# Keys and queries made inside the first gradient's program, Newton-Schulz with an early norm and without a rebuilt X

## The chip, the cores and the metric

The kernel runs on one core of a Trainium2 chip. The time is device microseconds (us) of one execution, the median of several. Five engines work side by side, each in its own order: TensorE (PE in the profile, its weight loads PEld), VectorE (DVE), ScalarE (ACT), GpSimd (POOL) and SyncE (SP, which only issues transfers here). They wait for each other by semaphores.

## What is computed

A hybrid transformer block on x of shape 4 x 512 x 128, so 2048 tokens, 16 tiles of 128. The change touches only the first of its four parts, a test-time-training attention:

```
q, k, v = split(layernorm(x) @ qkv_w + qkv_b)            # each 2048 x 128
q, k = q / (norm over 8 + 1e-6) * scale + bias           # 16 heads of 8
theta = gate, val (128 x 512), proj (512 x 128)
for _ in range(2):
    h = swish(k @ gate) * (k @ val); pred = h @ proj
    grads = d mean((pred - v)**2) / d theta
    theta -= 0.1 * newton_schulz(grads)                  # 3 matrices
o = (swish(q @ gate) * (q @ val)) @ proj @ proj_w + proj_b

newton_schulz(G): X = G / (norm(G) + 1e-7)
    5 times: A = X @ X.T; X = a*X + (b*A + c*(A @ A)) @ X
```

Then follow a mixture of 8 small experts, a block-causal attention and the experts again, which stay as they are.

## The kernel before

The program is a row of blocks; at the end of each all engines meet. `qkv_phase` makes q, k, v. Then, twice, `gradient_phase` and `schulz_phase`, and then `query_phase`.

**qkv_phase.** Each engine runs `pipeline`: step s does stage X of tile s minus its lag. ACT normalises a tile, PE turns and projects it (L315, L320), DVE adds the bias (`bias_add`, L348), ACT squares, DVE sums the squares of each head (L352), ACT takes the root and DVE inverts it, POOL multiplies by it (`unit`, L254) and by the scale (`scaled`, L261), DVE adds the shift (L367), PE turns the result (L325, L326) and ACT copies it to `qkT` and to `qkv`. Ahead of the first tile ACT copies a transposed `proj` (L269, L270) and only then loads the table for the layer norm's root (L179).

**gradient_phase.** All products with the weights of `forward` and `back` are three matmuls each (`mm3`): an operand is split into a part `h` that a fast format holds and the rest `l`. ACT makes `kh` from `qkT` and POOL the rest `kl`, per tile and again in each of the two gradients. PE's order for a step is turn_h, add_proj, forward, predict, add_gate, turn_d, add_val, back, with lags of 1 to 3 tiles; ACT does tanh, derive and two copies, DVE seven elementwise operations. Three PSUM banks (`acc`) gather the gradients.

**schulz_phase.** The three gradients (index m) go side by side. With P = c A A + b A + a I, an X that isn't touched gives X' = P X and A' = P A P. So the kernel keeps A (128 x 128) and a product Q of the Ps. A round is: square (PE), poly (DVE), times_a (PE), a copy T (ACT), next_a (PE), a mixture and a copy (DVE). After two rounds it rebuilds X and its transpose with Q (L695, L699), takes A from them anew (L653), and goes on with three rounds. Ahead of this the norm of G is read from the diagonal of G G^T, and X is turned by PE and copied by ACT. At its end gate, val and proj are updated and split again, with POOL making the rests of gate and val (L646).

**query_phase.** Splits q as above (`high`, `low`), 512 tokens at a time, and runs gate and up products (`gate_up`), a sigmoid, and an output product.

## Time and profile before

| | |
|---|---|
| median of 3 runs | 866.35 us (862.17 to 867.6) |
| the profiled execution | 866.14 us |
| its span, first to last instruction | 863.7 us |
| mean granted TensorE clock | 0.94 of full speed |
| PE, PEld busy | 90%, 71% |
| DVE, ACT, POOL busy | 63%, 46%, 31% |

The stages lie so in the span: q, k, v from 0 to 51.2 us; first gradient to 159.9; first Newton-Schulz to 196.0; second gradient to 306.7; second Newton-Schulz to 342.7; query to 393.7; the rest to 863.7. A busy time is the sum over a stretch; a share near 100% says that an engine had always something in work, not that it ran at its peak. In a timeline row the text in brackets is the idle time just before and what ended it. An fp32 product is recorded as two matmuls, so `x6` are three products.

### The profile page before, as it was taken

What the parts mean: (1) busy time and instruction counts of PE and PEld (TensorE: products, weight loads), DVE (VectorE), ACT (ScalarE), POOL (GpSimd) and SP (SyncE); (2) the same over time, 40 slices, a digit from 0 to 9 for tenths busy, and PEclk for the clock granted to TensorE, in tenths of its full rate; (3) what the DMA queues carried; (4) which work ended last, traced back from release to release, by engine and by line L of the source; (5) the groups of instructions that cost most, each with busy time, mean ns of one, the idle gap of its engine ahead of it and who ended that gap; (6) DMA issues with size and microseconds to landing.
All of it is one profiled execution on the core that took longest, in us unless ns stands there. A gap on an engine that the chain in (4) does not pass through costs nothing. (4 is left out here: it accounts for less than half of the span.)

```text
span 863.7 us, 15529 instructions
## 1 busy us (share of the span) xinstructions
PE 774.2 (90%) x5512; PEld 616.6 (71%) x5512; DVE 545.4 (63%) x1649; ACT 394.9 (46%) x1118; POOL 270.7 (31%) x476
## 2 busy tenths in 40 slices
PE   3669999897999988987858999999999999999786
PEld 1239999775999976677645677777777777777765
DVE  3945656444555535664796776776677666665468
ACT  4733333243333234312255766565556555564224
POOL 4830000002445002100372444343334333333027
PEclk9969999997999999895898999999999999999678
DMA  3040000000000000000000000000000000000001
GB/s 104 1 134 1 1 2 1 1 1 1 1 1 2 1 1 1 0 1 1 0 2 0 2 2 2 2 2 1 2 2 1 2 2 2 2 1 2 1 0 50
DMA packets 9466, 7.17 MB, mean 8 GB/s; under 512 B 1584, under 2 KB 9008, under 8 KB 9264
## 3 DMA queue, kind: packets, MB, share of 16 engines
q1 hardware_dynamic: 9392, 6.19, 2.3%
q8 instruction: 46, 0.75, 0.4%
q14 instruction: 28, 0.23, 0.1%
HBM read 5.14 MB, written 1.05 MB: 7 GB/s over the span
## 5 line engine op out<-in xcount | busy, mean ns | idle before, releaser
L1295 POOL TENSOR_SCALAR t_p_<-t_p_,t_rinv_ 128x128 f32<-128x128 f32 (+3 forms) x256 | 132.1, 532 | 202.3 <-DVE t_rinv_ L1491 202.3
L1325 ACT ACTIVATE t_p_<-t_p_,t_nmin_ 128x128 f32<-128x128 f32 (+3 forms) x256 | 140.0, 551 | 9.1 <-DVE t_nmin_ L1484 9.1
L1484 DVE CUSTOM_DVE_ANT_0 t_p_<-t_S_,t_mask_ 128x128 f32<-128x128 f32 (+3 forms) x256 | 112.8, 487 | 21.7 <-PE t_S_ L1382 17.3
L1330 ACT ACTIVATE t_pT_<-t_T_ 128x384 f32<-128x384 f32 (+1 forms) x96 | 50.5, 526 | 118.3 <-PE t_T_ L1394 118.3
L1394 PEld LDWEIGHTS t_T_<-ident,t_p_ 128*128 128x128 f32 x640 | 68.2, 141 | 44.9 <-issue 26.0
L1382 PE MATMUL t_S_<-t_k_,t_q_ 64*128 64x256 f32 (+3 forms) x512 | 95.0, 468 | 0.1
L1394 PE MATMUL t_T_<-ident,t_p_ 128*128 128x128 f32 x640 | 90.8, 281 | 0.3 <-ACT t_pT_ L1330 0.3
L1409 PEld LDWEIGHTS t_O_<-t_pT_,t_v_ 128*64 128x64 f32 x1280 | 69.2, 137 | 11.0 <-ACT t_pT_ L1330 10.5
L1409 PE MATMUL t_O_<-t_pT_,t_v_ 128*64 128x128 f32 x1280 | 76.9, 275 | 0.0
L522 DVE SCALAR_TENSOR_TENSOR g_sw<-g_th,g_G 128x512 f32<-128x512 f32 x32 | 22.0, 688 | 71.3 <-ACT g_slope L436 66.2
L1382 PEld LDWEIGHTS t_S_<-t_k_,t_q_ 64*128 64x128 f32 x512 | 41.5, 185 | 26.9 <-DVE t_nmin_ L1484 12.3
L1495 DVE COPY t_pT_<-t_T_ 128x384 f32<-128x384 f32 (+1 forms) x96 | 57.3, 597 | 1.4 <-PE t_T_ L1394 1.3
L408 POOL TENSOR_TENSOR g_kl<-qkT,g_kh 128x128 fp32r<-128x128 f32 x32 | 14.6, 457 | 138.0 <-ACT g_kh L427 138.0
L1500 DVE COPY t_oT_<-t_O_ 128x512 f32<-128x512 f32 x32 | 22.1, 691 | 54.8 <-PE t_O_ L1409 54.8
L1325 ACT ACTIVATION_READ_ACCUMULATOR t_p_<-t_p_,t_nmin_ 128x1 f32 x256 | 48.6, 190 | 0.0
L440 ACT ACTIVATE g_hT<-g_H 128x512 f32<-128x512 f32 x32 | 19.1, 597 | 60.0 <-PE g_H L472 60.0
L1037 ACT ACTIVATE m_y_<-m_A_,m_wt_ 128x128 f32<-128x128 f32 x96 | 28.0, 367 | 25.4 <-PE m_A_ L102 25.4
L646 POOL TENSOR_TENSOR gvl<-gv,gvh 128x512 fp32r<-128x512 f32 x4 | 5.0, 1273 | 104.3 <-ACT gvh L751 104.3
L479 PEld LDWEIGHTS g_PT<-proj,g_hT 128*128 128x128 f32 x256 | 33.8, 193 | 2.6
L498 PE MATMUL acc<-qkv,g_dg 128*128 128x128 f32 x256 | 34.0, 276 | 1.0 <-DVE g_dg L549 1.0
L479 PE MATMUL g_PT<-proj,g_hT 128*128 128x128 f32 x256 | 34.1, 276 | 0.0
L498 PE MATMUL acc<-qkv,g_du 128*128 128x128 f32 x256 | 33.8, 275 | 0.0
(259 smaller groups left out, 1794.5 us busy)
## 6 DMA issues: line engine op xcount, KB each, us to landing
wqkv<-in_L_attn_b_w_qkv_dram SPq DMA_DIRECT2D x1, 1536.0 KB
x<-in_L_attn_a_x_dram SPq DMA_DIRECT2D x4, 256.0 KB, 4.2
out_dram<-x SPq DMA_DIRECT2D x4, 256.0 KB, 2.3
we<-in_L_ffn_We_dram SPq DMA_DIRECT2D x1, 512.0 KB
wout<-in_L_attn_b_w_out_dram SPq DMA_DIRECT2D x1, 512.0 KB
proj<-n_L_attn_a_ttt_proj_dram SPq DMA_DIRECT2D x1, 256.0 KB, 5.3
gv<-n_L_attn_a_ttt_gate_dram SPq DMA_DIRECT2D x1, 256.0 KB, 4.9
gv<-in_L_attn_a_ttt_val_dram SPq DMA_DIRECT2D x1, 256.0 KB, 5.4
```

Source lines behind the costliest of these rows:

```text
L479: last = pe.matmul(pred, hT[:, t.ring, n * P:n * P + P], self.proj[:, n, :], start=(n == 0), stop=(n == NC - 1))
L498: last = pe.matmul(self.acc[:, n, m, :], src[:, t.ring, m * P:m * P + P], d[:, t.ring, :] if n == 2 else k, start=False, stop=False, skip_ ...
L1037: last = act.activation(y[:, t % 4, tile_of(k)], experts_of(t, e), ACT.Copy, scale=weight(t, e))
L1295: last = pool.tensor_scalar(pr[:, G.par, h, cols], pr[:, G.par, h, cols], rinv[:, G.par, n:n + 1], 1.0, ALU.mult, ALU.mult)
L1325: act.activation(pr[:, G.par, h, cols], pr[:, G.par, h, cols], ACT.Exp, bias=nmin[:, G.par, n:n + 1], scale=-1.0, accum_out=rsum[:, G.par, ...
L1330: act.activation(pT[:, G.par, 0, G.blocks], psT[:, 0, 0:G.width], ACT.Copy).then_inc(t["eA"], 1)
L1382: last = pe.matmul(psS[:, (2 * G.n + h) % 3, at_:at_ + (qt + 1) * P], qp[d, G.par, qt * P:qt * P + P], kp[d, G.par, 0:(qt + 1) * P], start ...
L1394: last = pe.transpose(psT[:, h, k:k + P], pr[:, G.par, h, at_:at_ + P], ident[:, :])
L1409: last = pe.matmul(psO[d, qt * P:qt * P + P], v[:, G.b % 2, n, G.p * P + h * DH:G.p * P + h * DH + DH], pT[:, G.par, h, at_:at_ + P], star ...
L1484: dve.tensor_tensor_reduce(pr[:, G.par, h, cols], psS[:, (2 * G.n + h) % 3, at_:at_ + keys], mask[:, SEQ - keys:SEQ], 1.0, -NEG, ALU.add, ...
L1495: dve.tensor_copy(pT[:, G.par, 1, G.blocks], psT[:, 1, 0:G.width]).then_inc(t["eB"], 1)
L1500: dve.tensor_copy(oT[:, b % 2, p, :], psO[:, :]).then_inc(t["oT"], 1)
```

## The change

Four things change. (1) `qkv_phase` is gone; a class `Front` does its work inside the first gradient's block, and its buffers are those of the gradient. ACT no longer copies `proj` ahead of the layer norm. POOL squares 6 of the 16 tiles, root and inverse are taken for 4 tiles at once, and POOL alone does the product with the inverse, the scale and the shift, in place in `qkv`. (2) The transposes of q and k (`turn_qk`) are a stage of the gradient's own pipeline, all other lags are one larger, and ACT (`high`) and DVE (`low`) split both once into `qkh` and `qkl`, which the second gradient and the query stage read. (3) In `schulz_phase` all five rounds run on A; Q is gathered beside them in a PSUM bank of its own; X is turned inside the rounds. A round's square and mixture become A times R with R = c A + b I, and a I is added on DVE. The norm comes from the squares of G, on ACT and DVE. (4) The activation table of the next stage is loaded in `schulz_phase`, and the second `schulz_phase` leaves out the updates that nobody reads (`proj`, `pTh`, `pTl`).

```diff
+class Front:
+    POOL_SQUARES = tuple(range(4, NT, 2))
...
+        def square(t):
+            pool.wait_ge(self.s["out"], t + 1)
+            pool.wait_ge(self.s["ss"], t - 3)
+            qk = k.qkv[:, t, 0:2 * P]
+            pool.tensor_tensor(self.sq[:, t % 4, :], qk, qk, ALU.mult).then_inc(self.s["sqp"], 1)
+        def unit(t):
+            heads = lambda ap: ap.rearrange("p (g d) -> p g d", d=QD)
+            qk = k.qkv[:, t, 0:2 * P]
+            pool.wait_ge(self.s["inv"], t // TPB + 1)
+            pool.tensor_tensor(heads(qk), heads(qk), self.ssq[:, t, :].unsqueeze(2).broadcast_to([P, 2 * QH, QD]),
+                               ALU.mult).then_inc(self.s["m"], 1)
+            pool.wait_ge(self.s["m"], t + 1)
+            pool.tensor_tensor(qk, qk, self.scale_all[:, :], ALU.mult).then_inc(self.s["s"], 1)
+            pool.wait_ge(self.s["s"], t + 1)
+            pool.tensor_tensor(qk, qk, self.shift_all[:, :], ALU.add).then_inc(self.s["k"], 1)
+        early = 0
+        for t in self.POOL_SQUARES:
+            square(t)
+            if t in (8, 12):
+                unit(early)
+                early += 1
+        for t in range(early, NT):
+            unit(t)
+            if t == early + 1:
+                pool.wait_ge(self.s["ptc"], 2)
+                pool.tensor_tensor(k.pTl[:, :], k.projT[:, :], k.pTh[:, :].bitcast(F32), ALU.subtract).then_inc(self.s["ptl"], 1)
...
+        def root(b):
+            of = slice(b * TPB, b * TPB + TPB)
+            act.wait_ge(self.s["ss"], TPB * (b + 1))
+            act.activation(self.ssq[:, of, :], self.ssq[:, of, :], ACT.Sqrt).then_inc(self.s["rt"], 1)
+        def keep_proj():
+            act.wait_ge(self.s["pt"], 1)
+            for dst in (k.projT, k.pTh):
+                act.activation(dst[:, :], self.psP[:, :, :].rearrange("p c d -> p (c d)"), ACT.Copy).then_inc(self.s["ptc"], 1)
+        for s in range(NT + 3):
+            if s < NT:
+                norm(s)
+            if 0 <= s - 1 < NT:
+                copy(s - 1)
+            if 0 <= s - 3 < NT and s - 3 not in self.POOL_SQUARES:
+                square(s - 3)
+            if s == NT:
+                keep_proj()
+            if s % TPB == 3 and TPB < s < NT:
+                root(s // TPB - 1)
+        take_first()
+        root(BATCH - 1)
...
+        def sumsq(t):
+            dve.wait_ge(*self.squares(t))
+            dve.tensor_reduce(self.ssq[:, t, :], self.sq[:, t % 4, :].rearrange("p (g d) -> p g d", d=QD),
+                              AX.X, ALU.add).then_inc(self.s["ss"], 1)
+        def invert(b):
+            of = slice(b * TPB, b * TPB + TPB)
+            dve.wait_ge(self.s["rt"], b + 1)
+            dve.tensor_scalar(self.ssq[:, of, :], self.ssq[:, of, :], 1e-6, None, ALU.add).then_inc(self.s["gd"], 1)
+            dve.wait_ge(self.s["gd"], b + 1)
+            dve.reciprocal(self.ssq[:, of, :], self.ssq[:, of, :]).then_inc(self.s["inv"], 1)
+        for s in range(NT + 3):
+            if 0 <= s - 1 < NT:
+                bias_add(s - 1)
+            if 0 <= s - 3 < NT:
+                sumsq(s - 3)
+            if s % TPB == 0 and s >= 2 * TPB:
+                invert(s // TPB - 2)
+        invert(BATCH - 1)
...
-                pipeline(act, (2, keep_hT), (0, k_high), (1, tanh), (1, derive), (2, dT_high))(base)
+                if front:
+                    act.sem_inc(g["hT"], 1)
+                    front.scalar(act, lambda: high(Tile(0, 0)))
+                    act.preload_act_table(ACT.Derivative_silu)
+                    pipeline(act, (3, keep_hT), (2, tanh), (2, derive), (3, dT_high), (1, next_high))(base)
+                else:
+                    pipeline(act, (2, keep_hT), (1, tanh), (1, derive), (2, dT_high))(base)
...
+                def turn_qk(t):
+                    pe.wait_ge(front.s["k"], t.done())
+                    pe.wait_ge(front.s["ptc"], 2)
+                    if t.number() != 0:
+                        pe.wait_ge(g["qkl"], t.done() - 1)
+                    for n in range(2):
+                        last = pe.transpose(turned[:, n, :], qkv[:, t.number(), n * P:n * P + P], self.ident[:, :])
+                    last.then_inc(g["T"], 1)
...
-                pipeline(pe, (2, turn_h), (3, add_proj), (1, forward), (2, predict), (3, add_gate), (2, turn_d),
-                         (3, add_val), (2, back))(base)
+                if front:
+                    pipeline(pe, (3, turn_h), (4, add_proj), (2, forward), (3, predict), (4, add_gate), (3, turn_d),
+                             (4, add_val), (3, back), (1, turn_qk))(base)
...
+                def low(t):
+                    dve.wait_ge(g["qkh"], t.done())
+                    dve.tensor_tensor(qkl[:, :, t.cols()], turned, qkh[:, :, t.cols()].bitcast(F32), ALU.subtract).then_inc(g["qkl"], 1)
...
+                    pipeline(dve, (2, swish), (3, error), (2, hidden), (3, dT_low), (2, gate_factor), (3, grad_val),
+                             (1, low), (3, grad_gate))(base)
...
+                gram(0)
+                gram(1)
+                pe.wait_ge(self.s_trace, 3 * step + 3)
+                pe.matmul(total, self.ones[:, :], tr[:, :], start=True, stop=True).then_inc(self.s_total, 1)
+                gram(2)
+                for k in range(K - 1):
+                    poly(k)
+                    times_a(k)
+                    if k < 3:
+                        turn(k)
+                    if k:
+                        gather(k)
+                    next_a(k)
+                poly(K - 1)
+                gather(K - 1)
...
-                square(0)
-                times_a(0)
-                next_a(0)
-                square(1)
-                last_q(1, lambda m: Pm[:, 0, m, :])
-                for m in range(3):
-                    pe.wait_ge(used[m], after(m, "q1"))
-                    for n in range(NC):
-                        last = pe.matmul(big[m][:, n, :], X[:, m, n, :], Q[:, m, :], start=True, stop=True)
-                    last.then_inc(made[m], 1)
-                for m in range(3):
-                    pe.wait_ge(used[m], after(m, "xt2"))
-                    pe.matmul(flat(big[m]), Q[:, m, :], flat(X[:, m, :, :]), start=True, stop=True).then_inc(made[m], 1)
-                for m in range(3):
-                    pe.wait_ge(used[m], after(m, "x2"))
-                    gram(m, XT2, "a2").then_inc(made[m], 1)
-                square(2)
-                times_a(2)
-                next_a(2)
-                square(3)
-                times_a(3, True)
-                next_a(3)
-                square(4)
-                last_q(4, lambda m: Q[:, m, :])
...
+                act.activation(junk[:, 0, :], flat(big[0]), ACT.Square, accum_out=tr[:, 0:1]).then_inc(self.s_trace, 1)
                 act.preload_act_table(ACT.Sqrt)
+                act.wait_ge(self.s_total, step + 1)
+                act.activation(nrm[:, :], total, ACT.Sqrt).then_inc(self.s_root, 1)
+                act.preload_act_table(ACT.Derivative_silu if again else ACT.Sigmoid)
+                act.wait_ge(self.s_nsv, 3 * step + 3)
                 for m in range(3):
-                    copy(m, flat(X[:, m, :, :]), flat(big[m]), "x")
-                act.wait_ge(self.s_norm, 4 * step + 4)
-                act.activation(nrm[:, :], small[0][:, 3, 0:3], ACT.Sqrt).then_inc(self.s_root, 1)
...
+                for k in range(K - 1):
+                    take(T, 2, f"t{k}")
+                    if k:
+                        take_q(k)
+                    take(A, 0, f"a{k}")
+                    if k < 3:
+                        take_x(k)
+                take_q(K - 1)
...
+                def factor(name):
+                    for m in range(3):
+                        dve.wait_ge(used[m], in_sbuf(name))
+                        dve.scalar_tensor_tensor(R[:, m, :], A[:, m, :], NS_C, bI[:, :], ALU.mult, ALU.add).then_inc(r_used[m], 1)
...
+                        dve.wait_ge(made[m], in_psum(f"p{k}"))
+                        dve.tensor_tensor(Pm[:, k % 2, m, :], small[m][:, 1, :], aI[:, :], ALU.add).then_inc(used[m], 1)
...
-                act.preload_act_table(ACT.Sigmoid)
...
-                        last = mm3(pe, ps_[:, n % 2, :], self.gvh[:, cols], self.gvl[:, cols], qh[:, b.ring, :], ql[:, b.ring, :])
+                        last = mm3(pe, ps_[:, n % 2, :], self.gvh[:, cols], self.gvl[:, cols],
+                                   self.qkh[:, 0, b.cols(SEQ)], self.qkl[:, 0, b.cols(SEQ)])
...
-            k.qkv_phase()
```

How the order moves at three places (L520 is predict, L541 the three add stages, L526 turn_d, L504 turn_qk, L513 turn_h in the changed file).

PE in the middle of the first gradient, before, from predict of one tile to turn_h of the next:

```order
L479 MATMUL g_PT<-proj,g_hT 128x128 x4
L498 MATMUL acc<-qkv,g_dg 128x128 x4
L485 MATMUL g_PT<-ident,g_d 128x128
L498 MATMUL acc<-qkv,g_du 128x128 x4
L100 MATMUL g_D<-pTh,g_dTh 128x512
L101 MATMUL g_D<-pTl,g_dTh 128x512
L102 MATMUL g_D<-pTh,g_dTl 128x512
L472 MATMUL g_H<-ident,g_h 128x128 x4
```

and in the changed kernel:

```order
L520 MATMUL g_PT<-proj,g_hT 128x128 x4
L541 MATMUL acc<-qkv,g_dg 128x128 x4
L526 MATMUL g_PT<-ident,g_d 128x128
L541 MATMUL acc<-qkv,g_du 128x128 x4
L100 MATMUL g_D<-pTh,g_dTh 128x512
L101 MATMUL g_D<-pTl,g_dTh 128x512
L102 MATMUL g_D<-pTh,g_dTl 128x512
L504 MATMUL g_PT<-ident,qkv 128x128 x2
L513 MATMUL g_H<-ident,g_h 128x128 x4
```

Two transposes per tile have moved from their own stage to the end of PE's step.

POOL in the front of the changed kernel (L179 squares, L185 product with the inverse, L188 scale, L190 shift):

```order
L179 TENSOR_TENSOR g_du<-qkv 128x256 x3
L185 TENSOR_TENSOR qkv<-qkv,g_ssq 128x256
L188 TENSOR_TENSOR qkv<-qkv,g_scale_all 128x256
L190 TENSOR_TENSOR qkv<-qkv,g_shift_all 128x256
L179 TENSOR_TENSOR g_du<-qkv 128x256 x2
L185 TENSOR_TENSOR qkv<-qkv,g_ssq 128x256
L188 TENSOR_TENSOR qkv<-qkv,g_scale_all 128x256
L190 TENSOR_TENSOR qkv<-qkv,g_shift_all 128x256
L179 TENSOR_TENSOR g_du<-qkv 128x256
```

The squares are those of tiles 4, 6 and 8, then 10 and 12, then 14; between them stand the three operations of tile 0 and of tile 1. Before, POOL had two operations a tile (L254, L261) and no squares.

PE in Newton-Schulz, the changed kernel, start and first two rounds (L726 poly, L731 times_a, L720 turn, L738 gather, L744 next_a):

```order
L714 MATMUL n_small<-n_XT 128x128 x8
L749 MATMUL n_side<-n_tr,ones 128x3
L714 MATMUL n_small<-n_XT 128x128 x4
L726 MATMUL n_small<-n_R,n_A 128x128 x3
L731 MATMUL n_small<-n_A,n_P 128x128 x3
L720 MATMUL acc<-ident,n_XT 128x128 x4
L744 MATMUL n_small<-n_T,n_P 128x128 x3
L726 MATMUL n_small<-n_R,n_A 128x128 x3
L731 MATMUL n_small<-n_A,n_P 128x128 x3
L720 MATMUL acc<-ident,n_XT 128x128 x4
L738 MATMUL n_side<-n_P 128x128 x3
L744 MATMUL n_small<-n_T,n_P 128x128 x3
```

The transposes of X and the product for Q now stand between times_a and next_a, and the three rows of the rebuild (L695, L699, L653) are gone.

## Rows read from the trace of the kernel before

**Rows 1.** Engine busy time by stretch: start, end and length in us, then busy time.

```profile
0.00:51.20 51.20, 24.56 (x84) 11.95 (x84) 32.76 (x105) 29.47 (x101) 34.77 (x47) 0.92 0.15 44
...
159.90:196.00 36.10, 29.81 (x190) 24.98 (x190) 17.39 (x62) 13.86 (x34) 2.50 (x2) 0.95 0.00 1
...
342.70:393.70 51.00, 43.66 (x232) 36.45 (x232) 31.76 (x56) 13.51 (x22) 5.87 (x4) 0.90 0.00 0
```

**Rows 2.** Timeline before the first bias addition: start, duration in us, engine, line.

```profile
9.29 0.17 DVE L170 TENSOR_SCALAR lnw<-lnw 128x16 f32<-128x16 f32 x1
...
11.70 1.28 ACT L179 ACT_TABLE_LOAD   x1
...
12.99 0.22 ACT L181 ACTIVATE lnw<-lnw 128x16 f32<-128x16 f32 x1
...
14.25 0.88 ACT L276 ACTIVATE p_xn_<-x,p_nmr_,rstd 128x128 f32<-128x128 f32 x2 [1.04 <-DVE p_nmr_ L338]
...
17.49 0.56 DVE L348 TENSOR_TENSOR qkv<-p_Q_,p_bias_ 128x384 f32<-128x384 f32 x1 [3.43 <-PE p_Q_ L320]
```

**Rows 3.** Instruction groups of the first 51.2 us: count, busy us, mean ns.

```profile
L261 POOL TENSOR_TENSOR p_sc_<-p_m_,p_scale_all_ 128x256 f32<-128x256 f32 x16 | 14.2, 893 | 0.0
...
L254 POOL TENSOR_TENSOR p_m_<-qkv,p_inv_ 128x256 f32<-128x256 f32 x16 | 10.8, 672 | 3.7 <-DVE p_inv_ L361 1.7
...
L348 DVE TENSOR_TENSOR qkv<-p_Q_,p_bias_ 128x384 f32<-128x384 f32 x16 | 8.1, 504 | 4.3 <-PE p_Q_ L320 4.3
...
L352 DVE TENSOR_REDUCE ssq<-p_sq_ 128x32 f32<-128x256 f32 x16 | 6.4, 397 | 0.0
```

**Rows 4.** Timeline of PE, first forward matmul of the first gradient.

```profile
53.55 0.77 PE L100 MATMUL g_G<-gvh,g_kh 128*128 128x512 f32 x1 [0.26 <-issue]
```

**Rows 5.** Timeline, first gradient in steady state: one tile's period and a DVE operation.

```profile
69.55 0.60 PE L472 MATMUL g_H<-ident,g_h 128*128 128x128 f32 x4
...
75.83 0.60 PE L472 MATMUL g_H<-ident,g_h 128*128 128x128 f32 x4
...
76.27 1.06 PE L498 MATMUL acc<-g_d,g_h 128*128 128x128 f32 x8
...
151.45 0.69 DVE L545 SCALAR_TENSOR_TENSOR g_du<-g_D,g_sw 128x512 f32<-128x512 f32 x1 [0.47 <-PE g_D L102]
```

**Rows 6.** Timeline of the first Newton-Schulz stage: its start, rounds and last product.

```profile
160.10 1.08 ACT L723 ACTIVATE n_XT<-acc 128x512 f32<-128x512 f32 x2 [5.08 <-PEq L383]
...
167.64 0.94 PE L659 MATMUL n_small<-n_A 128*128 128x128 f32 x6 [2.52 <-DVE n_T L778]
...
173.16 2.94 PE L695 MATMUL acc<-n_Q,n_X 128*128 128x128 f32 x24
...
182.00 0.94 PE L659 MATMUL n_small<-n_A 128*128 128x128 f32 x6 [0.64 <-DVE n_T L778]
...
183.40 0.72 ACT L723 ACTIVATE n_T<-n_small 128x128 f32<-128x128 f32 x3 [4.08 <-PE n_small L666]
...
183.73 0.94 PE L671 MATMUL n_small<-n_T,n_P 128*128 128x128 f32 x6
...
184.80 1.28 PE L659 MATMUL n_small<-n_A 128*128 128x128 f32 x6
...
190.22 2.31 PE L713 MATMUL acc<-n_X,n_Q 128*128 128x512 f32 x5
```

**Rows 7.** Timeline of PE, first forward matmul of the second gradient.

```profile
198.34 0.76 PE L100 MATMUL g_G<-gvh,g_kh 128*128 128x512 f32 x1 [1.11 <-ACT g_kh L427]
```

**Rows 8.** Timeline around the start of the query stage.

```profile
339.52 2.50 POOL L646 TENSOR_TENSOR gvl<-gv,gvh 128x512 fp32r<-128x512 f32 x2 [52.15 <-ACT gvh L751]
...
342.85 1.28 ACT L850 ACT_TABLE_LOAD   x1 [1.69 <-PEq L629]
...
342.89 1.68 PE L872 MATMUL q_W_<-proj_w,projT 128*128 128x128 f32 x8 [2.29 <-PEq L629]
...
345.97 0.79 PE L100 MATMUL q_G_<-q_qh_,gvh 128*128 128x512 f32 x1 [1.40 <-DVE q_ql_ L907]
```

544 lines of the change are left out of this document (237 added, 307 removed).

## The prediction

> **What bounds the kernel now.** I read first the busy times by stretch [rows 1]. The stretch of q, k and v (0 to 51.2 us) is half idle on every engine: PE 24.56 us, DVE 32.76, ACT 29.47, POOL 34.77 of 51.2, so waits between engines bound it. In the first Newton-Schulz stretch PE is busy 29.81 of 36.1 us, but with chains of three small products. In the query stretch PE has 43.66 of 51.0. Then the timeline at the places where the stages start. The first bias addition runs at 17.49 [rows 2]; the first forward product of the gradient at 53.55 [rows 4]. In the gradient one tile takes 75.83 - 69.55 = 6.28 us on PE without a gap [rows 5]: there PE is the bound, and work taken from other engines gives nothing. In Newton-Schulz a round with nothing beside it takes 184.80 - 182.00 = 2.80 us, while from 173.16 to 182.00, 8.84 us, X is rebuilt [rows 6]. The sum is made against the profiled execution, 866.14 us, 0.2 below the median of 866.35.
>
> **1. The front, to the first forward product.** ACT loaded the root's table at 11.70, behind the two copies of proj, and took the root at 12.99; its input was there at 9.29 + 0.17 and a semaphore, about 9.66 [rows 2]. The changed kernel loads the table at the very start and has nothing ahead of the root, so all that follows moves by 12.99 - 9.66 = 3.3 us: the first normalised tile from 14.25 to 10.9, the first bias addition from 17.49 to 14.2 [rows 2]. A tile costs DVE 0.504 + 0.397 = 0.90 us [rows 3]; ACT has less than before. So the bias of tile 8 is added 8 x 0.90 = 7.2 us later, plus about 1.5 for the first slow tiles and the first inversion: done at 22.9.
>
> From there POOL is the chain, because it has its tasks in a fixed order and DVE and ACT wait for its squares. Four squares (tiles 8, 10, 12, 14) and the operations of tiles 0 and 1 stand there. A square I price at 0.75, between the product with the inverse (0.672) and the one with the scale (0.893) [rows 3]; the three operations of a tile at 2.35, between 3 x 0.672 = 2.0 and 3 x 0.893 = 2.7, nearer the middle because one is of the first kind and two of the second, which slows only beside DVE. With 0.5 us of waiting for the bias of tile 12: 22.9 + 3.0 + 4.7 + 0.5 = 31.1. Then two sums of squares on DVE (0.8), the root on ACT (0.3), a wait of DVE for POOL to finish one operation and a short add (0.7), a reciprocal over 128 columns (0.45, between the sum's 0.397 and the bias addition's 0.504 [rows 3]) and the rest `low` of tile 0 (0.5): the first forward product at 33.9. Against 53.55 [rows 4] that is **-19.7 us**. The transposes of tile 0, the copies of proj and `high` are done by then, in ACT's and PE's waits; the table for tanh loads under the first forward product. The ends: with every POOL operation at 0.672 and no wait 32.2, so -21.3; with every one at 0.893 and twice the waits 37, so -16.5. What becomes late next is POOL's rest: tile 2 comes at about 33.5, then one tile in 2.35 us, while the gradient takes one in 6.5; pTl on POOL is ready at 37, `back` of tile 0 needs it at 43.
>
> **2. The first gradient.** PE gets two transposes a tile, each 0.11 us, for four take 76.27 - 75.83 = 0.44 [rows 5]. 0.22 x 14 tiles (the first two fall into gaps of the start) is **+3.1 us**. ACT's `kh`, POOL's `kl` go and ACT's `high`, DVE's `low` come: neither engine is the bound, 0. If that cover fails, see the last rival.
>
> **3. Newton-Schulz, twice.** Counted from its first copy (160.10), the first square product started at 167.64 - 160.10 = 7.5 us, the last product with X at 190.22 - 160.10 = 30.1 [rows 6]. Now: ACT's two copies 1.1 and its square 0.8, a table load 1.28, so the root ends at 3.3, while DVE's two sums end at 2.4 and the total is there at 3.0. A second table load ends at 4.6 (on the path, DVE's three small operations lie under it). Three copies of 128 columns take ACT 0.72 [rows 6], so one 0.28 and each further one 0.22. A copy of A 0.3, R on DVE 0.3: the first product at 5.25. A phase of three products, whose result another engine must take, lasts (183.73 - 182.00)/2 = 0.87 us; from product to ACT's copy 183.40 - 182.87 = 0.53, and from there 0.33 to the next product [rows 6] (182.87 being the middle of the two phases). Round 0: poly 0.87; times_a 0.66 and the turn of X 0.44, together 1.1; next_a, copy of A, R 1.2; in all 3.2. Rounds 1 and 2: 0.87; times_a 0.66, turn 0.44, gather 0.66, together 1.76; then ACT copies three Qs (0.9 from the last product of gather) before A, and A and R take 0.65: in all 4.2 each. Round 3 has no turn: 3.75. Round 4: 0.87 and gather, copy of Q 1.2. So 5.25 + 3.2 + 8.4 + 3.75 + 2.05 = 22.65, against 30.1: **-7.5 us**, twice. The ends: if Q's copies delay nothing and PE is never slowed, rounds 1 and 2 take 3.4 and -9.3; if PE falls to its lower clock in the rounds, as it did for some of this stage (0.95 granted [rows 1] is 0.05 x 2 x 36.1 = 3.6 us at 1.2 of 2.4 GHz), -5. The second stage also ends sooner: its last work is now POOL's gvl, 339.52 + 2.50 = 342.02, while the next program began at 342.85; with 0.28 between programs that is **-0.55** [rows 8].
>
> The table loads are where a rule speaks against the change. A load at 11.70 takes 1.28 us, and ACT's root begins at 12.99, 0.01 behind it [rows 2], so I count 1.28. The Trainium skill (ScalarE: Activation LUTs, What ACT_TABLE_LOAD costs) says that each switch costs another 1.38 us of drain, 2.66 in all; by it two loads in a row would cost each of the two stages 2.8 us more, and the sum would be 836.6. The trace does not agree: the 0.01 us leave no room for it.
>
> **4. Starts of the second gradient and the query.** The second gradient waited for a table load, `kh` and `kl` before its product at 198.34 [rows 7]; the zeroing products ahead of it end near 197.2: **-1.1**. The query stage's product came at 345.97, behind a table load and two rests on DVE; now it follows the product with proj_w, which ends at 342.89 + 1.68 = 344.57 [rows 8]: -1.4. Splits of later batches lay beside PE, 0; about 0.3 for a clock that rises earlier: **-1.7**. Ends: -0.8 and -2.2.
>
> **The sum.** -19.7 + 3.1 - 15.0 - 0.55 - 1.1 - 1.7 = -34.95, so 866.14 - 35 = **831 us**. Behind the query nothing is touched. All good ends together give about 825, all bad ones 841.
>
> **The rivals.**
> - *Newton-Schulz bound by ACT's queue or a low clock.* For: T, Q, A and X are all copied by ACT, 10 operations a round where it had 3 to 6. Each stage then gives 4.5 instead of 7.5: 837. Chance 0.14.
> - *ACT stands still behind a table load.* If two loads right behind other ACT work cost as long again as they take, 2 x 1.28 = 2.6 us in each stage: 836. Against: root and load lie 0.01 apart [rows 2]. Chance 0.03.
> - *POOL's front slower.* For: it now also adds the shift, and its operations already ranged from 0.672 to 0.893 beside DVE [rows 3]. At 1.2 us each the ten operations from tile 8 on take 12 instead of 7.7, forward starts at 38, with the waits at 40: 837. Chance 0.10.
> - *Clock better*: with less waiting PE starts the stages at its full clock. The query stretch has a granted 0.90 and the front 0.92 [rows 1]; half of the loss in the stages touched is 5 us: 826. Chance 0.09.
> - *Slower than before: `low` stands in the gradient's chain.* DVE's `low` waits for ACT's `high`, which waits for the transposes behind `back`, and `grad_gate` and all of DVE's next step stand behind it. It adds 0.22 + 0.25 + 0.4 + 0.5 us ahead of grad_gate (0.7, as [rows 5]), so dg is there 2.5 us after `back`; PE needs it after turn_h, one add, forward and predict, about 3.6 us. 1.1 us are free, so by these rows it costs nothing. It decides against the change if a tile takes 2.5 us longer than 6.5, for 14 x 2.5 = 35; with 3.1 it is 875. Chance 0.03.
> - *The front gains nothing*, since the first forward product waits for the last inversion anyway and every tile still pays: 857 to 860. Chance 0.02; the timeline above speaks against it.
>
> **The numbers.** The forecast has 0.59. The rivals at 837 to 838 have 0.27 together, the better clock 0.09. The range from 823 to 841 takes in the bounds of the terms and these cases, and leaves out about 0.15. A measurement of this kernel tells apart 1%, 8.7 us. Faster by more than that: 0.95, the four first cases and the forecast; within 1%: 0.02; slower: 0.03.
>
> **What would show it.** The first forward product between 32 and 37 us; POOL without a pause from the square of tile 8 to that of tile 14; a gradient tile in 6.5 us with PE still without gaps; the last product with X 22 to 24 us after the first copy of Newton-Schulz; the query's first gate product right behind the product with proj_w. I am wrong if ACT's queue holds up A for more than 1 us a round, if DVE waits in `low` long enough that PE waits for dg, or if the stages behind the query change their length.

## The result, and the profile of the changed kernel

The changed kernel takes 834.31 us (median of 4 runs, 833.25 to 834.65); the kernel before takes 866.98 beside it. The ratio is 0.9631, 95% interval 0.9602 to 0.966: 3.7% faster. Its profiled execution took 834.65 us, with a span of 832.8 and a mean granted clock of 0.95.

First the busy time by stretch, which answers to [rows 1] (start, end, length; then busy time of PE, PEld, DVE, ACT, POOL; granted clock, DMA share, GB/s). The rows are the front, the first two tiles of the first gradient, the first Newton-Schulz stage and the query stage.

```profile
0.00:37.00 37.00, 19.61 (x56) 9.86 (x57) 23.15 (x66) 18.55 (x52) 20.49 (x32) 0.94 0.45 139
37.00:51.00 14.00, 11.62 (x46) 9.25 (x47) 6.43 (x12) 4.41 (x9) 13.08 (x19) 0.67 0.01 2
151.30:174.00 22.70, 18.34 (x141) 16.52 (x141) 10.12 (x41) 14.17 (x49) 0.00 (x0) 1.00 0.00 1
...
314.50:362.90 48.40, 42.47 (x232) 35.66 (x232) 27.89 (x52) 10.16 (x18) 5.00 (x5) 0.93 0.00 1
```

In the front every engine is still idle for a third of the time or more. Behind it the clock is at 0.67 of full speed, which means at its lower level (1.2 of 2.4 GHz) for two thirds of these 14 us. In Newton-Schulz it is full throughout, where it was 0.95 [rows 1].

The timeline of the start, for [rows 2]:

```profile
8.77 0.22 ACT L211 ACTIVATE lnw<-lnw 128x16 f32<-128x16 f32 x1 [6.69 <-DVEq L390]
...
9.55 0.17 DVE L296 SCALAR_TENSOR_TENSOR g_nmr<-mean,rstd 128x16 f32<-128x16 f32 x1
9.76 0.88 ACT L217 ACTIVATE g_dg<-x,g_nmr,rstd 128x128 f32<-128x128 f32 x2 [0.77 <-DVE g_nmr L296]
...
12.96 0.56 DVE L301 TENSOR_TENSOR qkv<-g_H,g_th 128x384 f32<-128x384 f32 x1 [3.24 <-PE g_H L273]
```

The first bias addition comes 4.5 us sooner. Then the waits between 13 and 37 us (who waits, for whom: us in total, times, longest):

```profile
POOL g_du L179 <- DVE qkv L301: 8.5, 4, 3.2
ACT g_ssq L235 <- DVE g_ssq L305: 6.2, 4, 2.0
DVE qkv L301 <- PE g_D L273: 4.4, 4, 1.8
...
PE g_G L267 <- ACT g_dg L217: 1.7, 2, 0.9
```

POOL waits for DVE's bias additions, ACT's root (L235) for DVE's sums, PE for ACT's normalised tile (L217), and DVE for PE: a cycle, with POOL outside it. DVE's timeline around the first inversion shows what it costs there:

```profile
21.29 0.56 DVE L301 TENSOR_TENSOR qkv<-g_D,g_th 128x384 f32<-128x384 f32 x1 [1.06 <-PE g_D L273]
21.76 0.41 DVE L305 TENSOR_REDUCE g_ssq<-g_du 128x32 f32<-128x256 f32 x1
22.09 0.22 DVE L311 TENSOR_SCALAR g_ssq<-g_ssq 128x128 f32<-128x128 f32 x1
22.34 0.95 DVE L313 RECIPROCAL g_ssq<-g_ssq 128x128 f32<-128x128 f32 x1
23.21 0.49 DVE L301 TENSOR_TENSOR qkv<-g_H,g_th 128x384 f32<-128x384 f32 x1
```

And the end of the front, to the product that answers to [rows 4]:

```profile
34.41 0.68 DVE L305 TENSOR_REDUCE g_ssq<-g_du 128x32 f32<-128x256 f32 x2
...
35.13 0.31 ACT L235 ACTIVATE g_ssq<-g_ssq 128x128 f32<-128x128 f32 x1 [1.36 <-DVE g_ssq L305]
...
35.73 0.95 DVE L313 RECIPROCAL g_ssq<-g_ssq 128x128 f32<-128x128 f32 x1
...
36.60 0.36 DVE L566 TENSOR_TENSOR qkl<-g_PT,qkh 128x256 fp32r<-128x256 f32 x1
37.02 0.80 PE L100 MATMUL g_G<-gvh,qkh 128*128 128x512 f32 x1 [3.70 <-DVE qkl L566]
```

For [rows 5], PE in the steady first gradient, from one turn_h to the next: 6.66 us, with L504, the two transposes, ahead of turn_h.

```profile
69.22 0.60 PE L513 MATMUL g_H<-ident,g_h 128*128 128x128 f32 x4
...
73.84 1.06 PE L541 MATMUL acc<-qkv,g_du 128*128 128x128 f32 x8
74.90 0.47 PE L100 MATMUL g_D<-pTh,g_dTh 128*128 128x512 f32 x1
...
75.67 0.38 PE L504 MATMUL g_PT<-ident,qkv 128*128 128x128 f32 x2
75.88 0.60 PE L513 MATMUL g_H<-ident,g_h 128*128 128x128 f32 x4
```

For [rows 6], the first Newton-Schulz stage, which starts at 151.32: the table load, the poly products (L726) of the rounds, one copy of Q, the last product.

```profile
154.49 1.28 ACT L778 ACT_TABLE_LOAD   x1
155.78 0.88 ACT L783 ACTIVATE n_A<-n_small,n_r 128x128 f32<-128x128 f32 x3
156.60 0.94 PE L726 MATMUL n_small<-n_R,n_A 128*128 128x128 f32 x6 [1.46 <-DVE n_R L834]
159.76 0.94 PE L726 MATMUL n_small<-n_R,n_A 128*128 128x128 f32 x6 [0.25 <-DVE n_R L834]
162.71 0.61 ACT L793 ACTIVATE n_Q<-n_side 128x128 f32<-128x128 f32 x3 [0.83 <-PE n_side L738]
163.87 0.94 PE L726 MATMUL n_small<-n_R,n_A 128*128 128x128 f32 x6 [0.53 <-DVE n_R L834]
167.99 0.94 PE L726 MATMUL n_small<-n_R,n_A 128*128 128x128 f32 x6 [0.53 <-DVE n_R L834]
171.67 0.94 PE L726 MATMUL n_small<-n_R,n_A 128*128 128x128 f32 x6 [0.53 <-DVE n_R L834]
173.90 2.84 PE L764 MATMUL acc<-n_X,n_Q 128*128 128x512 f32 x6 [0.37 <-ACT n_Q L793]
```

For [rows 7] and [rows 8], the first products of the second gradient and of the query stage, the latter right behind the product with proj_w:

```profile
180.47 0.58 PE L100 MATMUL g_G<-gvh,qkh 128*128 128x512 f32 x1
...
314.57 1.13 PE L902 MATMUL q_W_<-proj_w,projT 128*128 128x128 f32 x8 [2.73 <-PEq L687]
...
315.46 0.48 PE L100 MATMUL q_G_<-qkh,gvh 128*128 128x512 f32 x1
```

### The profile page after: what moved, and what is told of

Read it like the earlier page. It is cut to its first block and busy times, and to the rows that moved or that the text cites. A ratio compares the mean times of both kernels' runs of the same rounds, so it can differ in the third digit from the quotient of the medians.

```text
span 832.8 us, 15217 instructions
## 1 busy us (share of the span) xinstructions
PE 754.0 (91%) x5430; PEld 602.5 (72%) x5432; DVE 529.5 (64%) x1587; ACT 381.5 (46%) x1080; POOL 267.2 (32%) x466
## 5 line engine op out<-in xcount | busy, mean ns | idle before, releaser
L520 PEld LDWEIGHTS g_PT<-proj,g_hT 128*128 128x128 f32 x256 | 34.0, 194 | 2.6
L541 PE MATMUL acc<-qkv,g_dg 128*128 128x128 f32 x256 | 34.0, 276 | 1.0 <-DVE g_dg L600 1.0
L454 ACT ACTIVATE g_th<-g_G 128x512 f32<-128x512 f32 x32 | 19.1, 598 | 34.1 <-PE g_G L102 34.0
L520 PE MATMUL g_PT<-proj,g_hT 128*128 128x128 f32 x256 | 34.4, 278 | 0.0
L596 DVE SCALAR_TENSOR_TENSOR g_du<-g_D,g_sw 128x512 f32<-128x512 f32 x32 | 22.1, 692 | 18.9 <-PE g_D L102 18.9
```

Source lines behind the costliest of these rows:

```text
L520: last = pe.matmul(pred, hT[:, t.ring, n * P:n * P + P], self.proj[:, n, :], start=(n == 0), stop=(n == NC - 1))
L541: last = pe.matmul(self.acc[:, n, m, :], src[:, t.ring, m * P:m * P + P], d[:, t.ring, :] if n == 2 else k, start=False, stop=False, skip_ ...
L596: dve.scalar_tensor_tensor(du[:, t.ring, :], psD[:, :], 0.5, sw[:, t.ring, :], ALU.mult, ALU.mult).then_inc(g["du"], 1)
```

## Where the time went, stage by stage

The same points of the program, read from the timelines of every kernel, give this table (us; with NS counted twice the columns add up to the span). "front" is from the first bias addition to the first forward product, "fill" from there to the second turn_h, "gradient 1" from there to the first copy of Newton-Schulz (14 tiles), "NS" to its last product with X (the two stages differ by 0.02 at most), "next" from that product to the first product of the next stage, twice.

| kernel | start | front | fill | gradient 1 | NS | next | gradient 2 | query and rest | span |
|---|---|---|---|---|---|---|---|---|---|
| before | 17.49 | 36.06 | 9.72 | 96.83 | 30.12 | 8.12, 5.92 | 108.49 | 520.81 | 863.7 |
| changed | 12.96 | 24.06 | 12.25 | 102.05 | 22.58 | 6.57, 5.57 | 105.95 | 518.23 | 832.8 |
| old Newton-Schulz | 13.27 | 23.18 | 10.64 | 101.99 | 29.27 | 6.37, 5.93 | 107.29 | 518.19 | 845.4 |
| A before Q | 12.95 | 24.58 | 10.64 | 101.99 | 20.41 | 6.57, 5.58 | 106.71 | 519.86 | 829.7 |
| no inverse | 13.17 | 19.63 | 11.36 | 101.96 | 22.58 | 6.57, 5.57 | 105.96 | 518.32 | 827.7 |
| waits once | 13.52 | 23.00 | 12.45 | 99.61 | 22.58 | 6.57, 5.57 | 107.24 | 518.28 | 831.4 |
| late root | 15.69 | 19.93 | 12.06 | 101.97 | 22.58 | 6.57, 5.58 | 105.96 | 519.98 | 832.9 |
| extra products | 13.22 | 24.59 | 9.95 | 101.97 | 22.59 | 6.55, 5.58 | 107.37 | 518.20 | 832.6 |
| no POOL squares | 13.62 | 24.96 | 10.63 | 101.95 | 22.59 | 6.57, 5.57 | 107.36 | 518.27 | 834.1 |
| load later | 13.01 | 22.53 | 12.11 | 102.04 | 21.92 | 6.98, 5.57 | 106.74 | 518.19 | 831.0 |
| inverse on POOL | 15.81 | 40.51 | 11.10 | 113.90 | 22.59 | 6.57, 5.58 | 107.14 | 516.52 | 862.3 |
| low early | 13.31 | 21.50 | 12.03 | 102.05 | 22.58 | 6.57, 5.58 | 107.35 | 518.15 | 831.7 |
| all edits | 13.53 | 19.00 | 12.41 | 99.64 | 19.74 | 6.57, 5.58 | 107.58 | 519.81 | 823.6 |
| all and products | 13.55 | 19.68 | 11.05 | 99.64 | 19.75 | 6.56, 5.57 | 106.75 | 519.80 | 822.1 |

"NS" and "gradient 1" repeat to 0.1 us from kernel to kernel wherever they are not edited (the inverse on POOL also reaches into gradient 1). The other columns move with nothing in them edited: "front" from 22.53 to 24.58, "fill" from 9.95 to 12.25, "gradient 2" from 105.95 to 107.58, "query and rest" from 516.52 to 519.98.

In the fill this is mostly the granted clock: 0.67 from 37 to 51 us in the changed kernel (fill 12.25), full from 33 us on in the kernel with extra products (9.95). The front goes with the clock too. In the changed kernel and in "A before Q" it was granted 0.79 from 25 to 33 us, and the front took 24.06 and 24.58; in the three other kernels whose front is as in the changed one (old Newton-Schulz, waits once, load later) it was full there, and the front took 23.18, 23.00 and 22.53. The two lines are those of the changed kernel and of "waits once":

```profile
25.00:33.00 8.00, 6.64 (x17) 3.33 (x19) 5.50 (x14) 5.05 (x16) 4.92 (x8) 0.79 0.01 3
25.00:33.00 8.00, 5.50 (x18) 2.54 (x19) 6.24 (x16) 5.39 (x18) 5.64 (x10) 1.00 0.00 1
```

So an edit is judged by its own column, and an edit of the front against 22.53 to 23.18 where its clock was full from 25 to 33 us. The medians of whole runs carry the movement of all the columns: of the single edits, only the old Newton-Schulz stage and the inverse on POOL have a ratio whose interval lies clear of the changed kernel's 0.9602 to 0.966.

## The experiments

All are edits of the changed kernel.

**1. The old Newton-Schulz stage.** The whole `schulz_phase` of the kernel before is put back, and two table loads with it:

```diff
+                    act.preload_act_table(ACT.Derivative_silu)
+                act.preload_act_table(ACT.Sigmoid)
```

> The changed kernel with the Newton-Schulz stage of the kernel before (rebuilt X, norm from the diagonal, all updates); the tables for the second gradient and the query stage are loaded at the start of those stages again. Theory: the two Newton-Schulz stages are independent of the rest and return 7.5 and 7.9 us, 849.7 us in all. If the cold clock at the start of the second gradient (0.50 granted from 198 to 206 us before, 1.00 now) came with the old rounds, another 2.5 us and 1.5 us of start come back: 853 to 854. Rival: the gain of these stages came from the operands split once and not from the rounds; then this kernel is near 838.

847.72 us (847.26 to 848.2), ratio to before 0.9786 (0.9769 to 0.9802). The stage takes 29.27, not 30.12: its granted clock is 1.00 here and was 0.94 before. So of the 7.5 us a stage that the change gained, the new rounds give 6.7 and the clock 0.85, and 847.72 - 834.31 = 13.4 us is 2 x 6.69. The starts of the second gradient (next 6.37) and of the query stage (518.19) stay as good as in the changed kernel, although both tables are loaded there again: those gains come from the operands split once, and the loads lie beside other work. The low clock at the start of the second gradient (0.50 from 198 to 206 us before) did not come back with the old rounds: gradient 2 takes 107.29, 1.3 more than in the changed kernel, no more than in others that have the new rounds. The value of 838 is excluded.

**2. A before Q.**

```diff
+                    next_a(k)
                     if k:
                         gather(k)
-                    next_a(k)
...
+                    take(A, 0, f"a{k}")
                     if k:
                         take_q(k)
-                    take(A, 0, f"a{k}")
```

> Newton-Schulz only: ACT copies A before Q, and PE makes the Q products after those for A. Theory: rounds 1, 2 and 3 of each stage lasted 4.11, 4.12 and 3.68 us against 3.16 of round 0, because A stands behind three copies of Q (0.72 us) on ACT and behind the Q products (0.4 to 0.66) on PE; each of them falls to 3.2 to 3.5, so 1.9 to 2.4 us a stage, 3.8 to 4.8 in all: 830 us. Rival: ACT has as much to copy as before in a round and is the bound, so that a round keeps 3.9 to 4.1 us: 834. Second rival: the last Q of a round now delays the T of the next: 1 us gained a stage, 832.3.

830.67 us (828.54 to 834.29), ratio 0.9593 (0.9563 to 0.9624). PE's poly products in the timeline of this kernel:

```profile
155.43 0.94 PE L726 MATMUL n_small<-n_R,n_A 128*128 128x128 f32 x6 [1.46 <-DVE n_R L834]
...
158.59 0.94 PE L726 MATMUL n_small<-n_R,n_A 128*128 128x128 f32 x6 [0.25 <-DVE n_R L834]
...
162.01 0.83 PE L726 MATMUL n_small<-n_R,n_A 128*128 128x128 f32 x6
...
165.33 0.83 PE L726 MATMUL n_small<-n_R,n_A 128*128 128x128 f32 x6
...
168.40 0.83 PE L726 MATMUL n_small<-n_R,n_A 128*128 128x128 f32 x6
```

Rounds 1 to 3 now take 3.42, 3.32 and 3.07 us, 2.1 less together, the stage 2.17 less, and PE no longer waits for DVE ahead of them. ACT was not the bound by its amount of work: with as many copies as before the rounds are shorter. The edit changes the order on ACT and on PE at once, so how much belongs to which of the two is not shown.

**3. No inverse.**

```diff
-            dve.wait_ge(self.s["gd"], b + 1)
-            dve.reciprocal(self.ssq[:, of, :], self.ssq[:, of, :]).then_inc(self.s["inv"], 1)
```

> The front without its four reciprocals (keys and queries are then multiplied by the root and not by its inverse; that part is left out). Theory: DVE is the bound of the front together with the waits it causes, so each 0.95 us reciprocal costs its length: the first forward product 3.8 us earlier, at 33.2, and with it the whole kernel: 830.5 us. Rival (the forecast's): POOL's fixed order is the chain; then only the last reciprocal counts, 0.95: 833.4.

830.59 us (828.11 to 833.45), ratio 0.9589 (0.956 to 0.9619). The front takes 19.63. Its clock was full from 25 to 33 us, so it stands against 22.53 to 23.18: 2.9 to 3.6 us less, 0.7 to 0.9 for each of the four reciprocals of 0.95 us. (Against the 24.06 of the changed kernel it is 4.4, but part of that goes with the clock.) The forecast's chain on POOL would have given back 0.95 in all.

**4. Waits once.**

```diff
-                    if front:
+                    if front and t.number() == 0:
                         pe.wait_ge(front.s["out"], NT)
```

This is turn_h; "ptl" in back and "ptc" in turn_qk are treated alike.

> PE waits for the front's last bias addition, for proj's copies and for the rest of proj only before the first tile, and not again before each of the 16. The first gradient's period is 6.65 us; two transposes explain 0.22 of the 0.37 added, and the product of back starts 1.06 us after add_val, where it was 0.90. Theory: the 0.15 is the time in which PE's sequencer goes through more wait instructions: period 6.50, 14 x 0.15 = 2.1 us less, 832.2 us. Rival: the 0.15 is DVE's low part of dT being late, or a changed order of DVE: period stays 6.65 and the time 834.3.

833.24 us (832.93 to 834.26), ratio 0.9622 (0.9602 to 0.9642). PE's timeline in this kernel:

```profile
73.07 1.06 PE L542 MATMUL acc<-qkv,g_du 128*128 128x128 f32 x8
73.97 0.47 PE L100 MATMUL g_D<-pTh,g_dTh 128*128 128x512 f32 x1
```

back starts 0.90 us after add_val again (1.06 above), the period is 6.48 instead of 6.65 on the mean of 14 tiles, and gradient 1 takes 99.61 instead of 102.05. Waits that had long been fulfilled cost 0.16 us a tile on the engine that is the bound, with no gap in its recorded busy time, whose ends are modelled. The rival (DVE late) is excluded, since DVE's order is untouched.

The whole 0.16 lies at one place, though. Ahead of back the distance from the last product of add_val falls from 0.28 to 0.12 us; turn_qk follows the last product of back after 0.23 us, and turn_h follows the second transpose after 0.11, with and without their extra wait. back has four waits in the changed kernel, turn_qk and turn_h three each. So two of the three waits cost nothing that can be seen. Whether it is the fourth wait in a row that costs, or something else about back, stays open, as no run takes out one wait alone.

**5. Late root.**

```diff
-            if s % TPB == 3 and TPB < s < NT:
-                root(s // TPB - 1)
+            if s % TPB == 0 and TPB < s:
+                root(s // TPB - 2)
```

> Front only: ACT takes the root of four tiles one step later, behind the next tile's normalisation and copy (the inversion on DVE stays where it is). Theory: ACT's wait for the sums at the root (1.23, 2.01 and 1.58 us) holds up the normalised tiles, PE waits for them and DVE for PE (1.06, 1.79 and 0.67 us idle): with the tile ahead of the root, DVE loses little and the way from the first bias addition to the first forward product falls from 24.06 to 21 to 22 us; 831.5 us. Rival: DVE's own work (16 x 0.9 us and 4 inversions of 1.1) is the bound, the root's place moves only where it waits: 23.5 to 24 us, 834.

833.73 us (831.66 to 834.71), ratio 0.9611 (0.9591 to 0.9631). The front takes 19.93: 4.1 less than in the changed kernel, but 2.6 to 3.2 less than in the fronts whose clock was full from 25 to 33 us, as it was here. That is what was expected (2 to 3) or a little more. From 20.4 to 33.7 us DVE has no idle time, and the root waits only for the last sums (1.42 us). The wait that cost was not DVE's own but that of the tile queued behind the root. In the profiled execution nothing of it arrives at the end, because its start is 2.7 us later and "query and rest" is 1.75 longer. The timeline of this kernel:

```profile
10.07 2.34 POOL L164 TENSOR_TENSOR gvh<-gv,ones 128x1024 fp32r<-128x1024 f32 x1 [6.25 <-DMA gv<-in_L_attn_a_ttt_val_dram]
10.19 2.25 DVE L296 SCALAR_TENSOR_TENSOR g_nmr<-mean,rstd 128x16 f32<-128x16 f32 x1
12.48 0.88 ACT L217 ACTIVATE g_dg<-x,g_nmr,rstd 128x128 f32<-128x128 f32 x2 [2.85 <-DVE g_nmr L296]
```

The DVE operation that took 0.17 us in the changed kernel takes 2.25 when POOL's split of gate and val began ahead of it, and ends with it. Which of the two is first depends on when two transfers land.

**6. Extra products.** PE is kept busy in the pause of 3.70 us before the first forward product:

```diff
                 def forward(t):
+                    if front and t.number() == 0:
+                        for _ in range(14):
+                            pe.matmul(self.acc[:, 0, :, :].rearrange("p c d -> p (c d)"), self.zeros[:, 0:P], self.zeros[:, :],
+                                      start=False, stop=False, skip_group_check=True)
```

> PE issues 14 more zero products (bf16, added into the sums) in the 3.70 us in which it waited for the first forward product. Theory: the granted clock falls in that pause and stays low to about 48 us (0.67 granted from 37 to 51); with the pause filled the first forward product takes 0.50 instead of 0.80, and from it to the second turn_h it takes 10.64 us, as in kernels whose clock was full, instead of 12.25: 832.7 us. Rival: at a low clock 14 products of 0.43 take 6 us and hold the forward product back by 2 to 2.5 us: 836.5. Second rival: the clock follows something else (the stall at 25 to 29 us, where it first fell), no change: 834.3.

834.7 us (832.01 to 835.35), ratio 0.9619 (0.9595 to 0.9644): no gain. The first half of the theory held: the clock is full from 33 to 54 us, the forward product takes 0.50, the fill 9.95 instead of 12.25. The second half did not: gradient 2 takes 107.37 instead of 105.95, with 0.90 granted from 184 to 200 us. Whether the one follows from the other is open. In several other kernels gradient 2 is as slow without this edit, and one with a cold fill (waits once, 12.45) has a slow gradient 2 as well.

**7. Load later.**

```diff
-                act.preload_act_table(ACT.Derivative_silu if again else ACT.Sigmoid)
...
                     act.activation(A[:, m, :], small[m][:, 0, :], ACT.Copy, scale=r2[:, m:m + 1]).then_inc(used[m], 1)
+                act.preload_act_table(ACT.Derivative_silu if again else ACT.Sigmoid)
```

> Newton-Schulz only: the table of the next stage is loaded behind ACT's three copies of A instead of ahead of them. Theory: the load of 1.28 us ends 1.5 us behind the root, while DVE's three small operations need 0.6 to 0.8: A comes 0.6 us sooner, the first product stands 4.7 instead of 5.28 us behind the start, and the load lies beside poly and times_a; 22.0 instead of 22.58 us to the last product in each stage, 833.2 us in all. Rival: the load now holds up the first copy of T, no gain; if a load also drained ACT for as long again, the stage would be longer by 0.7.

834.37 us (832.07 to 838.95), ratio 0.9652 (0.9616 to 0.9689). By the median nothing; by its column the stage takes 21.92 instead of 22.58, what was expected, twice. The 1.3 us do not stand out of a scatter of 7 us between its runs.

**8. No POOL squares.**

```diff
-    POOL_SQUARES = tuple(range(4, NT, 2))
+    POOL_SQUARES = ()
```

> Front only: all 16 squares on ACT, none on POOL. By the forecast POOL's fixed order (four squares and six operations after the bias of tile 8) is the chain of the front: freed of the squares, the first forward product comes 2 to 3 us sooner, 831.5 us. Theory now: POOL waits (3.19 and 2.79 us) for bias additions, and the cycle is DVE, ACT and PE; six squares of 0.42 us more on ACT make the way from the first bias addition to the first forward product 0.5 to 2.5 us longer, 24.6 to 26.5, and 835 to 837 us.

835.96 us (834.91 to 838.72), ratio 0.9645 (0.9624 to 0.9667). The front takes 24.96, longer and not 2 to 3 us shorter. Its clock was full to 37 us, so it is 1.8 to 2.4 us longer than the unedited fronts at that clock (22.53 to 23.18). The edit gives ACT more work as well; but POOL's waits of 8.5 us for DVE say the same: POOL was not the chain.

**9. The inverse on POOL.**

```diff
-            dve.tensor_scalar(self.ssq[:, of, :], self.ssq[:, of, :], 1e-6, None, ALU.add).then_inc(self.s["gd"], 1)
-            dve.wait_ge(self.s["gd"], b + 1)
-            dve.reciprocal(self.ssq[:, of, :], self.ssq[:, of, :]).then_inc(self.s["inv"], 1)
...
+                pool.tensor_scalar(self.ssq[:, of, :], self.ssq[:, of, :], 1e-6, None, ALU.add).then_inc(self.s["gd"], 1)
+                pool.wait_ge(self.s["gd"], b + 1)
+                pool.tensor_tensor(flat(self.ssq[:, of, :]), flat(self.ssq[:, of, :]), self.minus[:, :],
+                                   ALU.pow).then_inc(self.s["inv"], 1)
```

> Front only: the guard (+1e-6) and the inverse, as a power of -1, are taken on POOL right before it uses them; DVE has neither. POOL's power over 128 x 128 has no row in any trace here; bounds 0.4 us (its other operations on 128 columns) and 5 us. Theory: DVE is freed of 4 x 1.1 us, POOL hides the first two inverses in its waits of 3.19 and 2.79 us, the last is in the chain as before: if it costs about 1 us the first forward product comes 4 us sooner, 830.5 us. Rival: at 3 us or more each, POOL becomes the chain and tile 0 and the squares of 10 to 14 come later: 836 or more.

863.54 us (861.38 to 864.11), ratio 0.9954 (0.9935 to 0.9972): nearly the whole gain of the change is gone. The front takes 40.51 instead of 24.06, and gradient 1 another 11.85 us more, since POOL's later inverses run beside it. The start is also 2.85 us later, as in experiment 5. The timeline of this kernel has the first row for this operation:

```profile
26.61 20.81 POOL L192 TENSOR_TENSOR g_ssq<-g_ssq,g_minus 128x128 f32<-128x128 f32 x1
```

20.81 us, four times the upper bound that I had set and 22 times the reciprocal on DVE.

**10. Low early.** DVE's `low` of tile 0 moves from behind the last inversion to behind the third:

```diff
             if s % TPB == 0 and s >= 2 * TPB:
                 invert(s // TPB - 2)
+            if s == NT:
+                low_first()
```

> Front only: DVE takes the rest (low) of tile 0 before the last two sums of squares and the last inversion, which only tiles 12 to 15 need. Theory: the first forward product then waits for none of the two sums, the root, the add and the reciprocal: high ends at 33.8, the third reciprocal at 34.5, forward starts at 34.9 instead of 37.02 (from the first bias addition 22 instead of 24.06 us), and tanh is held to 37.1 by the table load: 832.5 us. Rival: the pause moves behind the first forward product, since ACT's root and table load come no sooner than 0.4 us later than before: the second turn_h comes at the same time, 834.3.

833.74 us (833.1 to 834.78), ratio 0.9632 (0.9611 to 0.9652). The front takes 21.50 instead of 24.06 and front and fill together 33.53 instead of 36.31; the median shows 0.6 of it. Little of this is the edit. PE's first turn_h, in the changed kernel and in this one:

```profile
41.46 1.09 PE L513 MATMUL g_H<-ident,g_h 128*128 128x128 f32 x4 [1.08 <-issue]
39.80 1.09 PE L515 MATMUL g_H<-ident,g_h 128*128 128x128 f32 x4 [2.70 <-issue]
```

The pause ahead of it grew by 1.6 us, as the rival said: ACT's table load still stands behind the last root, and tanh behind the load. And the clock was full here from 25 to 33 us; in the kernel with the old Newton-Schulz stage, whose front and fill have no edit, they take 33.82 together at that clock. Against that kernel the edit gives 0.3 us.

**11. All edits** (2, 4, 5, 7 and 10, and POOL's split behind the layer norm):

```diff
         pool.wait_ge(self.s["gv"], 32)
+        pool.wait_ge(self.s["shift"], 1)
```

> The changed kernel with six edits at once: A before Q in Newton-Schulz, table load behind the copies of A, PE's three waits of the front only before the first tile, the root one step later, low of tile 0 early, and POOL's split of gate and val not before the layer norm's last DVE operation (in one trace it began 0.12 us ahead of that operation, which then took 2.25 us instead of 0.17). From the traces: -4.1 and -1.5 to -2 in the front, -2.1 to -2.4 in the first gradient, -2.17 and -0.6 in each Newton-Schulz stage; the sum is -13.5, less what a cold clock takes back, so 821 to 824 us. Rival: each gain makes PE wait less evenly and the clock takes back as much as in the single edits (1 to 2 us each): 827.

823.58 us (819.92 to 825.4, 5 runs), ratio 0.9501 (0.9474 to 0.9529), against 0.9631 of the change alone; by the medians 10.7 us less. By columns: front -5.1 (3.5 to 4.2 against the unedited fronts at a full clock), gradient 1 -2.4, Newton-Schulz -2.84 twice; gradient 2 and the rest give back 1.6 each. The fill, at 12.41, is no shorter although its clock is better (0.88 from 37 to 51 us): PE now waits 3.12 us ahead of the first turn_h.

**12. All edits and the extra products** (11 and 6).

> The kernel with six edits, and the 14 zero products on PE in the pause before the first forward product. There the pause is 1.53 us, and the clock was full until it, then low from 38.4 us on (0.88 granted from 37 to 51). If the pause before the first forward product were what lowers the clock, the start of the gradient would be 1.5 to 2 us shorter: 822. Rival, from the kernel with this edit alone: 14 products take 3.2 us, longer than the pause, so the first forward product is 1.5 us later, and the clock gained here is lost in the second gradient (there 107.4 us instead of 105.95): 824 to 825.5.

822.13 us (818.91 to 823.91, 6 runs), ratio 0.9486 (0.9458 to 0.9514), not distinguishable from the eleventh. The fill is 1.4 shorter, the front 0.7 longer, and this time gradient 2 is not longer (106.75). The clock from 37 to 51 us is 0.88 as in the eleventh, so here the filled pause did not keep it up; what is shorter is the pause ahead of the first turn_h.

## Why the prediction was right, and where its terms were off

The forecast was 831 with 823 to 841, and 0.95 for faster; 834.31 came. By its own steps, between the two profiled executions (spans 863.7 and 832.8, so -30.9, against -34.95):

| step | forecast | measured |
|---|---|---|
| front, to the first forward product | -19.7 | -16.5 |
| first gradient | +3.1 | +7.75 (fill +2.53, 14 tiles +5.22) |
| Newton-Schulz, twice | -15.0 | -15.1 |
| end of the second stage | -0.55 | -0.35 |
| second gradient, its start included | -1.1 | -4.1 |
| query stage | -1.7 | -2.6 |

**Front.** 37.02 against 33.9, just outside the "between 32 and 37" that was to show it. The bad end of this term, 37, is also higher than its own rows give: with all ten operations at 0.893 and the waits of 0.5 and 0.7 doubled the sum comes to 36.3. The start was better than forecast (-4.5 instead of -3.3). Behind it the step "from there POOL is the chain" was wrong: POOL, which was to run without a pause, waits 8.5 us for DVE, and experiments 3, 5 and 8 show the cycle of DVE, ACT and PE instead. Two things were mis-sized or missed in it. The reciprocal over 128 columns was priced 0.45, between neighbours of other kinds, and takes 0.95, four times. And ACT's root was looked at for its 0.3 us only, not for the tile that stands behind it in ACT's queue while it waits. Another 0.9 to 1.5 us goes with the clock, 0.79 from 25 to 33 us, which the forecast had not in this term. The rival "POOL's front slower" gave 38 for a reason that did not occur. The rival "the front gains nothing" was put at 857 to 860; by the forecast's own terms, without the 19.7, it would be 851.

**First gradient.** The transposes cost 0.20 us a tile where 0.22 was forecast (6.48 in experiment 4 against 6.28 before). Missed were 0.16 a tile for PE's added waits (experiment 4), since I counted instructions that do work only, and 2.53 in the fill, of which 2.3 go with the clock (12.25 here, 9.95 at the full clock of experiment 6); the clock was forecast as a gain.

**Newton-Schulz.** Each part came as worked out: first product at 5.28 (5.25), rounds 3.16, 4.11, 4.12, 3.68 (3.2, 4.2, 4.2, 3.75), last part 2.23 (2.05). In part the -15.1 was owed to the clock, 0.85 a stage, which the forecast did not count as a gain here: the old rounds were measured at 0.94. The table load took its 1.28 us and ACT worked 0.01 us behind it (154.49 and 155.78); the rival with a drain is excluded.

**Second gradient and query.** The starts came 1.55 (-1.1 forecast) and 2.2 us sooner. The rest, 2.5 us in the second gradient, goes with the clock: it was 0.79 from 198.3 to 218 us before and 1.00 from 180.4 to 200 now, and a tile behind that takes 6.28 us in both. The rival "clock better" was right for this stage and wrong for the first. The errors of the front and the first gradient (+7.8) and of these stages (-3.9) partly cancel, so the total is nearer than its terms; that is luck.

**`low` in the gradient's chain** cost nothing, as its own working said.

## What to carry to other kernels

A task that waits in an in-order queue costs what stands behind it: put it where its input is sure to be there, and put the results that nobody needs soon (Q, the last inversion, a table) behind those on the chain. Waits that are always fulfilled are not always free on the engine that is the bound: here one of three places paid 0.16 us a tile. Take them once. Judge small edits by the length of their own stage in the trace: here medians of whole runs hid gains of 1.3 us (load later) and 1.4 of the 2.4 us of "waits once", because the clock and the first transfers vary by as much. But look at the stage's clock as well: the same front took 22.53 to 24.58 us, and an edit measured against one kernel alone (4.1 us for the late root, 2.8 for the early `low`) can be credited with what goes with the clock.

## What the hardware showed that was not expected

- A reciprocal on DVE grows steeply with its width: 0.25 us for 128 x 16, 0.34 for 128 x 32 (16 of them in the kernel before), 0.95 for 128 x 128, where an addition of a constant over the same 128 columns takes 0.22.
- A power on POOL over 128 x 128 takes 20.81 us (four of them, all within 0.01), against 0.63 for its product over 128 x 256.
- DVE can be held for a whole POOL operation. In two traces POOL's split (2.34 us) began 0.12 us ahead of a DVE operation on 16 columns, and that took 2.25 us; where DVE was first it took 0.17. In the kernel with all edits an addition of a constant takes 0.49 instead of 0.22 and ends 0.08 us after the POOL operation beside it; with `low` early two of them take 0.70 and 0.71 and end 0.08 and 0.09 after theirs. The Trainium skill (SBUF — State Buffer, Who interferes with whom) says that a DVE instruction with two SBUF inputs, or in a mode with two ports, and a GpSimd instruction that reads SBUF exclude each other for the whole instruction. The operation on 16 columns has two SBUF inputs, and its traces agree; that the addition ran in a mode with two ports no row here shows.
- The granted clock is part of a stage's price, but not of one place: with the same instructions the fill took 9.95 us where the clock was full and 12.25 where 0.67 was granted from 37 to 51 us, and the second gradient took 105.95 to 107.58.
